# A graph network layer pair on one core: tile 2 of the adjacency is loaded later and in two pieces, 44 warming products instead of 72, edge spreads behind tile 8, and low halves and mix rows moved

## What is computed

```python
def _L0(inst_feature, aggregator_matrix, rel_pair_index, Wq, bq, Wk, bk):
    q = (inst_feature[sub] @ Wq.T + bq).reshape(-1, HEADS, DK)
    k = (inst_feature[obj] @ Wk.T + bk).reshape(-1, HEADS, DK)
    att = ((q * k).sum(-1) / np.sqrt(DK)).T
    scores = zeros((HEADS, n, n)).at[:, sub, obj].set(att)
    scores = where(adj == 0, -inf, scores).at[:, di, di].set(1e-07)
    return softmax(scores, axis=2).sum(axis=0) / HEADS @ inst_feature

x = _layernorm(x + _L0(x, adj, ...))
x = _layernorm(x + (adj @ (x @ weight) + bias))
```

## Time and profile before

| | us |
|---|---|
| median of 3 runs | 165.84 (165.1 to 166.38) |
| the profiled execution itself | 166.42 |
| its span, first to last instruction | 164.7 |
| PE busy in the span | 153.4 |
| DVE busy in the span | 126.9 |
| ACT, POOL busy | 74.0, 70.5 |

### The profile page before, as it was taken

How to read it: one execution, slowest core, us unless ns; L and a number is a source line. 1 busy time by engine, 2 the same in 40 slices (tenths; PEclk the granted TensorE clock), 3 DMA queues, 4 the chain that set the end, 5 groups by cost and what they waited for, 6 DMA issues and landing times.

```text
span 164.7 us, 2902 instructions
## 1 busy us (share of the span) xinstructions
PE 153.4 (93%) x1024; PEld 79.9 (49%) x1025; DVE 126.9 (77%) x391; ACT 74.0 (45%) x125; POOL 70.5 (43%) x83
## 2 busy tenths in 40 slices
PE   3989999999999999999979999999999999999950
PEld 3934445455454445444434486444665444444530
DVE  2997889994899999999557988798991568666681
ACT  5687459845864412874191044153112104333451
POOL 7588777777777777787604434000020000000000
PEclk9999999999999999999999999999999999999997
DMA  4999889999259999651002730000001992312233
GB/s 124 388 379 343 318 230 336 379 408 364 81 143 358 320 345 380 221 119 39 0 0 49 186 143 6 0 0 0 0 0 24 337 299 106 131 69 71 88 127 127
DMA packets 16232, 28.99 MB, mean 176 GB/s; under 512 B 4769, under 2 KB 5953, under 8 KB 16086
## 3 DMA queue, kind: packets, MB, share of 16 engines
q1 hardware_dynamic: 10742, 24.14, 42.1%
q10 hardware_dynamic: 3280, 3.07, 5.5%
q0 software_dynamic: 2192, 1.57, 4.1%
HBM read 19.83 MB, written 8.58 MB: 173 GB/s over the span
## 4 chain that ended last, share of the span: by engine, by line
PE 38%; POOL 34%; issue 11%; DVE 9%; DMA 3%; ACT 1%; POOLq 0%; DVEq 0%
POOL ed_adj L647 29%; PE acc L1374 15%; PE acc L1464 13%; POOL found L655 5%; PE tr L1464 3%; DMA found<-in_adj,top_i 2%; PE tr L1416 2%; DMA ed_i<-in_pairs 1%; PE acc L1489 1%; DVE st L895 1%; DVE y L831 1%; PE acc L1378 1%; PE tr L1453 1%; ACT y L807 0%; PE tr L1429 0%
## 5 line engine op out<-in xcount | busy, mean ns | idle before, releaser
L647 POOL DMA_INDIRECT ed_adj<-in_adj,ed_idx x47 | 48.5, 1033 | 15.8 <-issue 14.0
L1374 PE MATMUL acc<-adjT,x1s 128*128 128x512 f16 (+1 forms) x240 | 49.3, 354 | 0.0
L1306 PE MATMUL acc<-xs,adjT 128*128 128x512 f16 (+1 forms) x176 | 40.6, 379 | 0.5 <-DVE xs L868 0.5
L1374 PEld LDWEIGHTS acc<-adjT,x1s 128*128 128x128 f16 x240 | 22.8, 98 | 21.1 <-issue 0.2
L1306 PEld LDWEIGHTS acc<-xs,adjT 128*128 128x128 f16 (+1 forms) x176 | 16.3, 98 | 20.0 <-DVE xs L868 2.0
L1464 PE MATMUL acc<-whl,xs 128*128 128x512 f16 (+1 forms) x108 | 23.8, 370 | 0.0
L1464 PEld LDWEIGHTS acc<-whl,xs 128*128 128x128 f16 x108 | 10.5, 98 | 11.8
L1306 PE MATMUL tr<-xs,adjT 128*128 128x512 f16 (+1 forms) x66 | 15.2, 379 | 0.0
L698 ACT CAST adjT<-stage 128x1408 f16<-128x1408 f32 x9 | 12.3, 1362 | 6.0 <-DMA stage<-in_adj_T 5.8
L751 ACT ACTIVATE xs<-acc 128x512 f16<-128x512 f32 (+1 forms) x12 | 6.2, 538 | 11.2 <-PE acc L1378 11.2
L686 POOL DMA_INDIRECT x_dram<-wraw,back_i x1 | 1.3, 1337 | 21.5 <-DVE wraw L1224 21.5
(11 more groups left out here) (283 smaller groups left out, 230.7 us busy)
## 6 DMA issues: line engine op xcount, KB each, us to landing
stage<-in_adj_T SPq DMA_DIRECT2D x9, 704.0 KB, 7.3
x_dram<-x_sb SPq DMA_DIRECT2D x10, 256.0 KB
x_sb<-in_x SPq DMA_DIRECT2D x3, 768.0 KB, 7.2
sums_dram<-y ACTq DMA_DIRECT2D x6, 256.0 KB, 6.7
sums_dram<-xd ACTq DMA_DIRECT2D x5, 256.0 KB, 7.1
x_sb<-x_dram SPq DMA_DIRECT2D x1, 1280.0 KB, 12.2
out<-y SPq DMA_DIRECT2D x5, 256.0 KB, 2.0
stage<-in_adj_T SPq DMA_DIRECT2D x3, 384.0 KB, 5.6
```

The costliest lines, as they stand in the source:

```text
L647: nc.gpsimd.indirect_dma_start(out=ed_adj[0:EP, c:c + 1], out_offset=None, in_=adj_flat, in_offset=bass.IndirectOffsetOnAxis(ap=ed_idx[0:E ...
L1306: last = mm(sum_bank(i)[:, :], adjT[0:width[k], k, i * P:(i + 1) * P], xs[0:width[k], half, k, :], start=(k == 0 and half == 0), stop=(k = ...
L1374: mm(mix_bank(u)[:, 0:j - i], x1s[:, half, k, f * P:(f + 1) * P], adjT[:, k, i:j], start=(k == 0 and half == 0), stop=False)
```

## The change

At the start tile 2 is no longer queued straight behind x: SP first stores the leftover edges, waits for the third part and loads tile 2 in two pieces, of 6 and 5 blocks, which ACT casts and PE uses separately. The warming products go from 72 to 44. `edge_bits` and `edge_keys` move between the low halves of x. The two spreads move behind tiles 8 and 9, and the packed words of a tile use four banks in place of two.

```diff
-            load_adj(2)
             sp.wait_ge(edges_split, 2)
             sp.dma_start(row_dram.rearrange("(c p) -> c p", c=LEFT), row16[:]).then_inc(row_stored, 16)
             sp.dma_start(col_dram.rearrange("(c p) -> c p", c=LEFT), col8[:]).then_inc(col_stored, 16)
+            sp.wait_ge(first_loaded[2], 16)
+            sp.dma_start(stage[:, 2, 0:AHEAD * P], adj_t[2][:, 0:AHEAD * P]).then_inc(ahead_loaded, 16)
+            sp.dma_start(stage[:, 2, AHEAD * P:NP], adj_t[2][:, AHEAD * P:NP]).then_inc(adj_loaded[2], 16)
             load_adj(3)
+            sp.wait_ge(adj_loaded[2], 16)
             load_adj(4)
             load_adj(5)
             load_adj(6)
+            load_adj(7)
+            load_adj(8)
             sp.wait_ge(row_stored, 16)
             sp.dma_start(hot[:, :], row_dram.partition_broadcast(P)).then_inc(row_spread, 16)
-            load_adj(7)
+            load_adj(9)
             sp.wait_ge(col_stored, 16)
             sp.dma_start(cols[:, :], col_dram.partition_broadcast(P)).then_inc(col_spread, 16)
...
-            cast_adj(2)
+            act.wait_ge(ahead_loaded, 16)
+            nc.scalar.copy(adjT[:, 0:AHEAD, 2 * P:3 * P], stage[:, 2, 0:AHEAD * P].rearrange("p (k i) -> p k i", i=P)).then_inc(ahead_cast, 1)
+            act.wait_ge(adj_loaded[2], 16)
+            nc.scalar.copy(adjT[:, AHEAD:T, 2 * P:3 * P], stage[:, 2, AHEAD * P:NP].rearrange("p (k i) -> p k i", i=P)).then_inc(adj_cast, 1)
...
-            for u in range(3):
+            for u in range(2):
                 mix_high(u)
             act.wait_ge(w1_loaded, 16)
             nc.scalar.mul(whl[:, 0], w1_raw, WS).then_inc(w1_hi, 1)
+            mix_high(2)
...
             mix_high(6)
+            act.wait_ge(base_shift, 1)
+            nc.scalar.activation(kk, kk, ACT.Identity, bias=st[:, 0, 9:10], scale=st[:, 0, 8:9]).then_inc(base_ready, 1)
...
             for t in range(T):
                 split_x(t)
+                if t == 2:
+                    edge_bits()
+                if t == 5:
+                    edge_keys()
             for t in range(2):
                 fold(t)
             coefs((0, 1))
-            edge_keys()
-            edge_bits()
...
+            def low_w1(k):
+
+                dve.wait_ge(w1_hi, 1)
+                V.scalar_tensor_tensor(whl[:, 1, k], w1_raw[:, k], WS, whl[:, 0, k], ALU.mult, ALU.subtract).then_inc(w1_lo, 1)
...
+                low_bias()
+                low_w1(0)
                 dve.wait_ge(top_found, 16 * TOP)
...
+            dve.wait_ge(slot_root, 1)
+            scale_shift(norm_a).then_inc(base_shift, 1)
             mix_low(6)
...
             mix_low(7)
-            dve.wait_ge(slot_root, 1)
-            step(scale_shift(norm_a))
-            step(V.tensor_scalar(kk, kk, norm_a[:, 8:9], norm_a[:, 9:10], ALU.mult, ALU.add))
...
-            keep_warm(72)
+            keep_warm(44)
...
-            mix_rows(0, 35)
+            mix_rows(0, 40)
             pe.wait_ge(flags_ready, 1)
...
-            mix_rows(72, 95)
+            mix_rows(77, 96)
             pe.wait_ge(shares_ready, 1)
```

More of the change, by code:

```diff
@@ L29 @@
 WORDS_BEFORE = {2: (2,), 3: (3,), 4: (4,), 5: (5, 6), 6: (7, 8), 7: (9, 10)}
-CASTS_AFTER = {0: (4,), 1: (5,), 2: (6,), 3: (7, 8), 4: (9,), 5: (10,)}
+CASTS_AFTER = {0: (4,), 1: (5,), 2: (6,), 3: (7, 8), 4: (9, 10)}
+AHEAD = 6
 LOOKS_IN = {8: (0, 1, 2, 3), 9: (4, 5, 6, 7)}
@@ L524, in sum_bank, with word_bank @@
             return (acc[0], acc[1], tr[2])[i % 3]
+        def word_bank(t):
+            return (tr[0], tr[1], acc[2], acc[4])[t % 4]
         def mix_bank(u):
@@ L565, in _ @@
             load_adj(6)
+            load_adj(7)
+            load_adj(8)
             sp.wait_ge(row_stored, 16)
             sp.dma_start(hot[:, :], row_dram.partition_broadcast(P)).then_inc(row_spread, 16)
-            load_adj(7)
+            load_adj(9)
             sp.wait_ge(col_stored, 16)
             sp.dma_start(cols[:, :], col_dram.partition_broadcast(P)).then_inc(col_spread, 16)
-            for t in range(8, T):
-                load_adj(t)
+            load_adj(10)
             sp.dma_start(bias_row[:, :], b1.rearrange("(o h) -> o h", o=1)).then_inc(bias_row_loaded, 16)
@@ L871, in fold @@
             def fold(i):
-                bank, new = tr[i % 2], fold_in[:, i % 2, :]
+                bank, new = word_bank(i), fold_in[:, i % 2, :]
                 dve.wait_ge(words_done, i + 1)
@@ L1142, in _ @@
             step(V.tensor_scalar(gone, keep, -1.0, -GONE, ALU.add, ALU.mult))
+            low_w1(2)
             dve.wait_ge(dots_done, 1)
@@ L1164, in _ @@
             step(V.tensor_copy(score[:, :, SLOTS + 2], sc))
+            low_w1(3)
             dve.wait_ge(scores_spread, 1)
@@ L1291, in words @@
                 for k in ks:
-                    last = mm(tr[t % 2][:, 0:WP + 1], adjT[:, k, t * P:(t + 1) * P], bit_eye[:, k, :], start=(k == 0), stop=(k == T - 1))
+                    last = mm(word_bank(t)[:, 0:WP + 1], adjT[:, k, t * P:(t + 1) * P], bit_eye[:, k, :], start=(k == 0), stop=(k == T - 1))
                 if ks[-1] == T - 1:
@@ L1298, in all_words @@
                 pe.wait_ge(adj_cast, t - 1)
-                pe.wait_ge(words_folded, t - 1)
+                if t >= 4:
+                    pe.wait_ge(words_folded, t - 3)
                 words(t, range(T))
@@ L1344, in select @@
                     last.then_inc(selected, 1)
-            for i in range(2, T):
+            pe.wait_ge(ahead_cast, 1)
+            words(2, range(AHEAD))
+            sum_neighbours(2, range(AHEAD), range(2))
+            pe.wait_ge(adj_cast, 1)
+            words(2, range(AHEAD, T))
+            sum_neighbours(2, range(AHEAD, T), range(2))
+            for i in range(3, T):
                 for t in WORDS_BEFORE.get(i, ()):
                     all_words(t)
-                if i >= 3:
-                    pe.wait_ge(y_ready, i - 2)
+                pe.wait_ge(y_ready, i - 2)
                 looks = LOOKS_IN.get(i, ())
@@ L1401, in _ @@
             last.then_inc(xobj_T, 1)
-            mix_rows(53, 56)
+            mix_rows(58, 61)
             pe.wait_ge(xsub_in, 16)
@@ L1407, in _ @@
             last.then_inc(xsub_T, 1)
-            mix_rows(56, 59)
+            mix_rows(61, 64)
             def project(bank, n, rows_T):
@@ L1424, in _ @@
             project(tr[1], 0, xsT).then_inc(q_done, 1)
-            mix_rows(59, 64)
+            mix_rows(64, 69)
             pe.wait_ge(qk_read, 1)
@@ L1430, in _ @@
             last.then_inc(dots_done, 1)
-            mix_rows(64, 72)
+            mix_rows(69, 77)
             pe.wait_ge(scores_ready, 2)
@@ L1446, in _ @@
             last.then_inc(change_T, 1)
-            mix_rows(124, 129)
+            mix_rows(125, 130)
             pe.wait_ge(dT_lo, 1)
-            pe.wait_ge(w1_lo, 1)
+            pe.wait_ge(w1_lo, KF)
             both = [dT[:, k].rearrange("p a s -> p (a s)") for k in range(KF)]
```

21 lines of the change are left out of this document (12 added, 9 removed).

## The result

| | before | after |
|---|---|---|
| median of 6 runs each, us | 165.13 (164.75 to 166.38) | 167.43 (166.65 to 169.04) |
| the profiled execution itself, us | 166.42 | 167.11 |
| its span, us | 164.7 | 165.4 |

The ratio is 1.0142, with an interval of 1.0101 to 1.0183: the change makes the kernel slower by 1.4%, 2.3 us in the medians. I had said 165.9 us, no change. The two profiled executions lie only 0.7 us apart.

A forecast was written before the change was run, and what follows sets the result against it. PE's chain of work was taken as the bound (busy 153.4 of 164.7 us). Mixed product +0.38, the change's wait -0.10 and the end -0.28 summed to 0.0 us: 165.9 us, no change, range 164.9 to 166.9.

The forecast's parts named there:

- The wait of 1.32 us goes.: Before the numbering: five more rows (2.16 us) cover PE's wait for DVE's flags, counted as -1.32 us of idle time.
- the new share wait: At line 1439's product (1475 after): fewer products cover DVE's share weights, so PE waits 1.9 us where 0.22 were.
- rival 4: At the start: PE idles with 44 warming products and falls to 1.2 GHz; 167.9 us, slower by 1.2%; chance 0.08.
- the spreads behind tile 8: On ACT: moving them frees its waits for tiles 7 and 8, but PE waits for neither; 0 us.
- the warming products at 0: At the start: 28 fewer only make PE wait longer for the same low half of x; 0, bounds 0 and -0.84 us.
- tile 2 without a wait: At PE's entry to tile 2: casting in two pieces removes the 0.43 us wait; bounds 0 and 0.43.
- no wait at the numbering: PE comes to the numbering at 84.93, when the flags are already there at 84.33.
- the low halves of weight and bias: Put into DVE's waits: 0 on the path; the fourth piece may pass its wait by up to 0.1 us.
- tile 2's start: PE enters tile 2 earlier by 0.24 us: the 0.43 wait goes, and low 8 takes 0.2 of it.

The follow-up runs named there:

- run 5: The kernel before with 19 in place of 23 mix rows between the spread of scores and the share product; 166.01 us, ratio 1.004.
- run 9: The changed kernel once more, with no further edit; 167.21 us, ratio 1.0035 to the kernel before.
- run 12: The kernel before once more, unedited, for its trace; 166.34 us.
- run 4: The kernel before with only the new stretches of mix rows; 167.5 us, ratio 1.0111.
- run 2: The changed kernel with the spreads back behind tiles 6 and 7 and tile 10's cast behind the sixth norm; 168.18 us, ratio 1.0153.
- run 11: The kernel before with 44 in place of 72 warming products and nothing else; 166.45 us, ratio 0.9971.
- run 10: The changed kernel with 28 unread products of 128 columns in the wait before the share product; 166.79 us, ratio 1.0046 to the kernel before.
- run 7: The kernel before with one index instruction (line 829) done five times, to make the flags late; 170.74 us, ratio 1.0248.
- run 6: The changed kernel with 22 in place of 19 mix rows between scores and shares; 165.91 us, ratio 1.0012 to the kernel before.
- run 1: The changed kernel with only the stretches of mix rows put back as before; 164.97 us, ratio 0.9976 to the kernel before.
- run 3: The changed kernel with both the spreads and the mix rows put back; 165.19 us, ratio 1.0003 to the kernel before.

## Why the prediction was wrong

The forecast's sum was +0.0, made of the terms below.

**The step that failed: "The wait of 1.32 us goes."** It does go, but I booked it as a gain of 1.32 us in every execution. Where the index step is short the flags are there when PE comes: run 5 starts the numbering at 83.01 without a wait, with before's code up to the scores. And in the changed kernel there is nothing left to gain even with the long step, since the gathers then end earlier (82.76 in run 9, where I had kept the 83.65 of the old trace). The term is worth 1.3 us in an execution like the first trace, 0.7 in one like run 12, and nothing in one like runs 4 or 5. How many of before's executions are of which kind is not shown, since both that were profiled had the long step; the gap between them and the median speaks for many short ones. I had the warning in hand. The profiled execution lay 0.6 us above the median of its three runs (1.3 above that of all six), I wrote it down, and I took 0.1 of it off. The right reading was: if the trace is slower than the median, a wait in it that hangs on a transfer is the first candidate for the excess, and a usual execution does not have it to give. By this reading the sum is 0 - (-1.32) = +1.3 us on a median of 165.1, that is 166.4, against 167.4 measured.

**Right: the new share wait.** Forecast 1.9 us at line 1475's product, measured 1.8, 1.8 and 1.7 (the change, runs 2 and 4); run 5 gave the size that its rows have. Counting the rows against DVE's chain of 8.54 us was sound. One count in it was off: before had 30 products of 512 columns there and not 29 (8 + 1 + 20 + 1), a cover of 8.4 and not 8.2 us, on which the new wait does not hang.

**Missed: the clock behind that wait.** I had the mechanism as rival 4, but put it at the start with its sparse products. There, 12 products of 512 columns take 2.94 us in the change and 2.75 in before and run 11, nowhere near 0.4 us apart. The low means go with the share wait instead. This, and the look's wait below, are what the runs offer for the 1.0 us that the mended sum leaves; how much of it is whose, no run separates. Rows only, run 4, cost 2.5 us in the medians of all: its quickest execution is 1.3 above before's median, not far from the 1.5 by which the wait has grown, and half of its executions had the lower mean clock and lie higher. In which stretch the clock was low in those executions no trace here shows, since none of them was profiled; that filling the pause removes them is run 10's evidence (none of 12, against 3 of 12 beside it), and the half pace behind a pause is seen in runs 7 and 11 alone, behind longer ones.

**Missed: the look behind its table**, 1.2 us in the change's trace, 0.7 to 1.0 in those of runs 6, 9 and 10, none in run 1. I had written that the spreads behind tile 8 cost nothing, because PE waited for neither tile. On the other side of the spreads, tiles 9 and 10 come later. ACT's casts stand ahead of its normalising step for tile 4, and the table is behind that:

```profile
44.11 1.37 ACT L709 CAST adjT<-stage 128x1408 f16<-128x1408 f32 x1 [2.36 <-DMA stage<-in_adj_T]
45.38 0.81 ACT L756 ACTIVATE x_sb<-y,st 128x512 f32<-128x512 f32 x1
```

In run 1 the same cast starts at 42.99 and the look doesn't wait, with the same order of the spreads: so this wait varies with when the tiles arrive. Putting the spreads back (runs 2 and 3) was not faster, as the tile casts before them then wait. The term was not zero, but its net is within what was measured.

**Right:** the warming products at 0 (run 11: 10.29 for the first low product); tile 2 without a wait; no wait at the numbering; the low halves of weight and bias, which delay nothing beyond the bound of 0.1 us (the third piece starts at 102.53, behind the end of POOL's casts at 101.39; the fourth lets DVE take the scores 0.60 us behind PE's product and not 0.50). The step of 1.79 us beside POOL's cast in the earlier trace rows now starts ahead of the cast, at another time, and takes 0.68:

```profile
96.91 0.68 DVE L1155 SCALAR_TENSOR_TENSOR xo<-wraw,xo 64x512 f16<-64x512 f32 x1
```

**Off:** tile 2's start. I forecast -0.24, and it was -0.86 in the trace. With the long step, as in the trace that I had worked from, run 9 has tile 2 at 19.50, that is -0.29; but run 11, which keeps tile 2 as before, has it at 19.50 as well, as its cast came in time. With the short step before's start has it at 19.63 and 19.64 (runs 4 and 5), and the changed one at 18.67 to 19.32 (the change, runs 1, 3, 6 and 10). So the short step alone is worth some 0.15 us, and the edits at the start 0.3 to 1.0 on top, which the wait at the look takes back.

No version beat before beyond doubt. The best is run 1, the change without its new rows: 0.9976, with an interval that holds 1. Of the changed kernel it is the faster by some 1.6% by the first comparison (1.0142 against 0.9976), and by 0.6% if run 9's 1.0035 is taken.

Left open: how often before's flags are late, as only a few executions were profiled, and whether the order of DVE's and POOL's early steps alone decides it, which an edit that forces that order would test.

## What to carry to other kernels

Before work is moved so that it covers a wait, ask whether a usual execution has that wait: compare the profiled execution with the median, and where it is slower, take the wait that hangs on a transfer out of the gain and give it as a bound. A cover that is taken from another chain costs in every execution: count that chain (here 8.54 us) against the products left (6.8 us) and treat the difference as certain. Before a step of an engine is moved, look also at what its old place held up on another engine: here four small DVE instructions between the low halves went with a shorter gather on POOL, and so with earlier flags. A pause of TensorE can have a second price, the clock behind it: pauses of 2.35 and 3.1 us were followed by half pace here, so of two places for idle time the one that is empty in most executions is the better.

## What was unexpected of the hardware

- One DVE instruction, 128 x 158 in fp32, took 0.24 us in some executions and 1.26 or 1.27 in others, and nothing in between was seen. It was long in the five traces in which it started behind a POOL instruction of 1.30 us (an iota of 128 x 1408), and then ended some 0.1 us after it.
- The third of POOL's gathers took 2.20 us, 4.0 or 5.81, most others 0.94, and in all traces it ended some 0.8 us after the first break in DVE's run of two-input fp32 subtractions (three, six and nine in a row).
- Behind a PE idle time of 3.1 us the granted clock stayed at 0.50 for about 6 us under dense products (run 7); behind 2.35 us, 12 products took 4.44 us (run 11), where at full clock they take 12 x 0.216 = 2.6. Kernels with a wait of 1.7 or 1.8 us had a mean granted clock under 0.985 in 12 of 36 executions, and none was seen in the 48 of kernels where it is at most 1.1 us or filled.
- 28 products of 128 columns that nobody reads, put into the wait, did not delay the share product, and the spread of the times was 1.2 us in place of 2.8 in 12 executions each.
